# A routed expert block after attention: the last three attention units written out, two banks for turned probabilities, place tables made ahead

## What is computed

```python
z = layernorm(x); z = layernorm(z) * ln_w + ln_b
q, qx, k, v = z @ wq, z @ wqx, z @ wk, z @ wv       # 16 query heads, 8 groups of d = 128
kx, vx = split(ctx @ w_kv_x)                        # q, qx, k and kx are normalised over d
core, xout = gqa(q, k, v), gqa(qx, kx, vx)          # softmax(q @ k.T / sqrt(d)) @ v
x = x + tanh(g_xattn) * (concat(core, xout) @ wproj)
h = layernorm(x)
p = softmax(30 * tanh((h @ w_gate) / 30))           # 8 experts, the top 2 of them for each token
y = sum(p[e] * ((silu(h @ w1[e]) * (h @ w3[e])) @ w2[e]) for e in top2(p))
out = x + tanh(g_ffn) * y
```

## Time and profile before

| | us |
|---|---|
| median of three runs | 717.48 |
| the profiled execution | 719.06 |
| its span, from the first to the last instruction | 717.3 |
| PE busy | 644.7 (90%) |
| DVE busy | 602.9 (84%) |
| ACT busy | 548.0 (76%) |
| POOL busy | 460.1 (64%) |

### The profile page before, as it was taken

How to read it: one execution, slowest core, us unless ns; L and a number is a source line. 1 busy time by engine, 2 the same in 40 slices (tenths; PEclk the granted TensorE clock), 3 DMA queues, 4 the chain that set the end, 5 groups by cost and what they waited for, 6 DMA issues and landing times. The chain is left out here.

```text
span 717.3 us, 14819 instructions
## 1 busy us (share of the span) xinstructions
PE 644.7 (90%) x4548; PEld 589.8 (82%) x4549; DVE 602.9 (84%) x1379; ACT 548.0 (76%) x1923; POOL 460.1 (64%) x636
## 2 busy tenths in 40 slices
PE   1677999999999999999999999999976569999994
PEld 0577889999998999999899999999965448888883
DVE  7579899999999999998999998987876697776771
ACT  4787979998988998998899899888854136656660
POOL 4666677687777778877777787787643124545442
PEclk9989999999999999999999999999999659999998
DMA  6100100010020101002010110100392512232322
GB/s 218 59 1 31 60 1 30 2 59 31 1 61 1 31 2 60 31 1 60 1 32 3 51 42 1 60 1 2 120 397 100 179 64 45 45 58 44 58 31 29
DMA packets 35509, 37.72 MB, mean 53 GB/s; under 512 B 2704, under 2 KB 30352, under 8 KB 35440
## 3 DMA queue, kind: packets, MB, share of 16 engines
q1 hardware_dynamic: 31024, 30.84, 13.0%
q0 software_dynamic: 4416, 6.03, 5.2%
HBM read 31.62 MB, written 5.24 MB: 51 GB/s over the span
## 5 line engine op out<-in xcount | busy, mean ns | idle before, releaser
L1192 POOL TENSOR_SCALAR shared<-shared,rsum 128x256 f32<-128x256 f32 x256 | 143.5, 573 | 67.1 <-DVE rsum L856 61.7
L615 ACT ACTIVATE shared<-s,nmax 128x256 f32<-128x256 f32 x256 | 122.5, 498 | 34.3 <-DVE nmax L851 34.2
L861 DVE TENSOR_TENSOR pt_lo<-t,pt_hi 128x512 fp32r<-128x512 f32 x128 | 86.9, 679 | 9.2 <-ACT pt_hi L621 8.3
L1186 POOL TENSOR_TENSOR rstd<-rstd,half 128x7 f32<-128x7 f32 (+1 forms) x64 | 91.2, 1425 | 5.3
L851 DVE TENSOR_REDUCE nmax<-s 128x2 f32<-128x512 f32 x128 | 86.6, 678 | 5.3 <-PE s L364 4.6
L375 PE MATMUL t<-ident,shared 128*128 128x128 f32 x512 | 78.0, 275 | 8.8 <-DVE pt_lo L861 5.6
L621 ACT CAST pt_hi<-t 128x512 fp32r<-128x512 f32 x128 | 76.4, 597 | 12.3 <-PE t L375 10.0
L629 ACT ACTIVATE shared<-route_bank,head_w 128x512 f32<-128x512 f32 (+1 forms) x124 | 81.6, 690 | 0.3 <-PE route_bank L389 0.3
L846 DVE TENSOR_TENSOR qk_lo<-shared,qk_hi 128x512 fp32r<-128x512 f32 x96 | 78.5, 817 | 3.0 <-POOL qk_hi L1201 1.9
L364 PE MATMUL s<-qk_hi 128*128 128x256 f32 x256 | 78.0, 305 | 0.6 <-ACT shared L615 0.6
L320 PE MATMUL pj_a<-w_ring,xq 128*128 128x256 f32 x488 | 73.8, 295 | 2.2 <-DVE w_ring L927 2.2
(11 more groups left out here) (255 smaller groups left out, 1927.9 us busy)
## 6 DMA issues: line engine op xcount, KB each, us to landing
expert_w<-in_w SPq DMA_DIRECT2D x24, 512.0 KB, 9.3
spare<-in_wT SPq DMA_DIRECT2D x19, 256.0 KB, 3.0
wp_raw<-in_wpT SPq DMA_DIRECT2D x16, 256.0 KB, 2.9
spare<-in_wkvT SPq DMA_DIRECT2D x16, 128.0 KB, 3.1
spare<-in_wT SPq DMA_DIRECT2D x9, 128.0 KB, 3.2
spare<-in_x SPq DMA_DIRECT2D x1, 1024.0 KB, 5.6
x_hat<-acc SPq DMA_DIRECT2D x1, 1024.0 KB, 4.7
out<-spare SPq DMA_DIRECT2D x1, 1024.0 KB, 7.9
```

The costliest lines, as they stand in the source:

```text
L615: e = act.activation(probs[:, st, h * S:(h + 1) * S], s_bank[st][:, h * S:(h + 1) * S], ACT.Exp, bias=nmax[:, st, h:h + 1], accum_out=psum ...
L861: dve.tensor_tensor(pt_lo[:, :, c], pt_bank[:].rearrange("p (n s) -> p n s", n=4), pt_hi[:, :, c].bitcast(F32), ALU.subtract).then_inc(ptl ...
L1186: pool.tensor_tensor(rstd[:, st, c], rstd[:, st, c], half[:, c], ALU.pow).then_inc(rstd_ready, 1)
L1192: m = pool.tensor_scalar(probs[:, st, c], probs[:, st, c], rsum[:, st, h:h + 1], 1.0, ALU.mult, ALU.mult)
```

## The change

1. **Units 29 to 31 are written out** on PE, ACT, DVE and POOL, in another order than `step` gives. In the units 30 and 31 the blocks with st = 1 are turned into `pj_a`, which has no projection left to hold, so `turn_probs` there waits for the block before the last. Some waits are added: `probs_hi` of these units for the values before, `split_heads` and `heads_hi` for the scores before.
2. **The last batch goes by tiles of 128 tokens**: `HATS` has five parts (three batches of two tiles, then one and one). `out_project` of unit 31 writes to the two score banks, `accumulate_last` reads one tile each. `choose` and `rank` go in three parts, `RANKED` (tiles 0 to 3, 4 and 5, 6 and 7).
3. **Place tables of six tiles ahead**: `first_places` (DVE) works out the places of the tiles 0 to 5 within their experts' last 128 before the starts of the experts are known, and POOL makes their twelve 128x128 tables, before the barrier. After it DVE makes those of the last two tiles only, and `id_slot`, which POOL made.
4. **The expert part**: `slot_expert` is worked out ahead of the tokens, `rows_rest(0, 0)` ahead of the scales, `hidden(0, 0, 0)` ahead of `rank_last`. In the loop `turn_hidden(n)` stands between the halves of `hidden(n + 1)` and `down(n)` behind them, where `down(n - 1)` stood between them; ACT and DVE follow.

```diff
+        def turned(u, a, st):
+
+            late = isinstance(u, int) and u >= U - 2 and st == 1
+            return pj_a if late else pt_bank
...
-            for u in range(1, U):
+            for u in range(1, U - 3):
                 step(u // B, u // B % 2, u % B)
...
+                two = isinstance(u, int) and f > 4 * (U - 2)
                 if above(f, 0):
-                    pe.wait_ge(ptlo_done, f)
+                    pe.wait_ge(ptlo_done, f - 1 if two else f)
...
+            turn_probs(31, 1, 0)
+            out_project(G - 1, 1, 2, 30, 0)
+            turn_probs(31, 1, 1)
+            out_project(G - 1, 1, 2, 30, 1)
+            values(31, 3, 1)
             turn_hat(0)
             turn_hat(1)
-            for st in range(ST):
-                out_project(G - 1, 1, B - 1, U - 1, st)
+            logits(0)
+            logits(1)
             turn_hat(2)
...
+            out_project(G - 1, 1, 3, 31, 0, s_bank[0][:, 0:H])
+            out_project(G - 1, 1, 3, 31, 1, s_bank[1][:, 0:H])
...
             def probs_hi(u, a, st):
                 act.wait_ge(pt_done, 4 * u + 2 * a + st + 1)
+                if u > U - 4:
+                    act.wait_ge(pv_done, 2 * u + a)
...
+            hat_copy(0)
+            smooth(G - 1, 31, 1)
+            hat_copy(1)
+            soft_cap(0)
...
+            def accumulate_last(st):
+                dve.wait_ge(tile_out, st + 1)
+                a = acc[:, NT - ST + st, :]
+                dve.tensor_tensor(a, s_bank[st][:, 0:H], a, ALU.add).then_inc(acc_read, 1)
...
+            def first_places():
+
+                dve.wait_ge(counted, 2)
+                n = NT - ST
+                c = slice(0, n)
+                for j in range(TOP):
+                    m = dve.scalar_tensor_tensor(early_pick[:, j, c], route.bank[:, NT * E:(NT + n) * E]
+                                                 .rearrange("p (t e) -> p t e", e=E), -(P - 1) / 2.0, route.pick[:, j, c], ALU.add, ALU.mult)
+                place_link(m)
+                place_link(dve.tensor_reduce(early_row[:, :, c], early_pick[:, :, c], AX, ALU.add))
+                place_link(dve.tensor_scalar(early_slot[:, :, c], early_row[:, :, c], ROWS, ROWS, ALU.add, ALU.subtract))
+                dve.tensor_tensor(early_row[:, :, c], early_row[:, :, c], early_slot[:, :, c], ALU.subtract).then_inc(early_placed, 1)
...
+            pool.wait_ge(early_placed, 1)
+            for t in range(NT - ST):
+                for j in range(TOP):
+                    m = pool.tensor_scalar(early_at[:, j, t, :], route.table[:, T_PLACE:T_PLACE + P], early_row[:, j, t:t + 1], 1.0,
+                                           ALU.is_equal, ALU.mult)
+            m.then_inc(route.places_set, 1)
...
             turn_rows(0, 0)
+            hidden(0, 0, 0)
             rank_last()
-            hidden(0, 0, 0)
             turn_rows(1, 1)
...
                 if more:
                     hidden(n + 1, 1 - par, 0)
-                if least(n, 1):
-                    down(n - 1, 1 - par)
+                turn_hidden(n, par)
                 if more:
                     hidden(n + 1, 1 - par, 1)
-                turn_hidden(n, par)
+                down(n, par)
...
-            for n in range(0, TOP * NT, QUARTER):
-                dve.tensor_tensor(at_place[:, n:n + QUARTER, :],
...
+            for part, v in enumerate((table[:, T_TILE:T_TILE + TOP * NT], off_place[:])):
+                m = dve.tensor_tensor(id_slot[:, part], at_slot[:], over_slots(v), ALU.mult)
+            m.then_inc(identified, 1)
...
+            def step(n, par):
                 more = not isinstance(n, int) or n + 2 < SLOTS
                 if more:
                     rows_rest(n + 2, par)
                     e = expert_of(n + 2)
-                    for i in range(2):
-                        weights_rest(n + 2, par, e, i)
-                if least(n, 1):
-                    take_y(n - 1, 1 - par)
+                    weights_rest(n + 2, par, e, 0)
+                if not isinstance(n, int) or n + 1 < SLOTS:
+                    take_hidden(n + 1, 1 - par)
+                if more:
+                    weights_rest(n + 2, par, e, 1)
+                take_y(n, par)
...
-            pool.wait_ge(sloted, 1)
-            pool.tensor_tensor(id_slot[:, 0], at_slot[:], table[:, T_TILE:T_TILE + TOP * NT].rearrange("p (n o) -> p n o", o=1)
```

More of the change, by code:

```diff
@@ L409, in out_project @@
                         pe.wait_ge(wp_ready, g + 1)
-                    if above(u, 0):
+                    if above(u, 0) and not last:
                         pe.wait_ge(acc_read, u)
@@ L555, in rank @@
                         pe.matmul(to, route.ones[:], route.chosen[:, earlier, :], start=earlier == 0, stop=False)
-                    pe.matmul(to, route.before[:], route.chosen[:, t, :], start=t == 0, stop=True)
+                    m = pe.matmul(to, route.before[:], route.chosen[:, t, :], start=t == 0, stop=True)
+                m.then_inc(counted, 1)
+            steps(step)
+            scores(29, 1, 0, 0)
+            turn_probs(28, 1, 0)
+            out_project(G - 2, 0, 3, 27, 1)
+            scores(29, 1, 0, 1)
@@ new lines, in _ @@
+            turn_heads(30, 2, 0)
+            turn_probs(28, 1, 1)
+            project_q(31, 1, 3, 0)
+            project_kv(31, 1, 3, 0)
+            scores(29, 1, 1, 0)
+            turn_probs(29, 0, 0)
+            values(28, 0, 1)
+            turn_heads(30, 2, 1)
+            scores(29, 1, 1, 1)
+            project_q(31, 1, 3, 1)
+            turn_probs(29, 0, 1)
+            turn_heads(30, 2, 2)
+            project_kv(31, 1, 3, 1)
+            scores(30, 2, 0, 0)
+            values(29, 1, 0)
@@ L1120, in step @@
                 row_sum(u, 1, 1)
-            steps(step)
             chain = [0]
@@ new lines, in _ @@
+            steps(step)
+            quantise(28, 0)
+            normalise_q(30, 2, 1)
+            row_max(29, 0, 0)
+            probs_lo(28, 1, 0)
+            normalise_kv(30, 2, 1)
+            row_max(29, 0, 1)
+            split_heads(29, 1, 2)
+            row_sum(29, 0, 0)
+            probs_lo(28, 1, 1)
+            row_max(29, 1, 0)
+            split_heads(30, 2, 0)
+            row_sum(29, 0, 1)
+            accumulate(27, 3)
+            normalise_q(31, 3, 0)
+            row_sum(29, 1, 0)
@@ L1165, in _ @@
+            probs_lo(31, 1, 1)
+            accumulate(30, 2)
+            x1_tiles(2)
+            quantise(31, 1)
+            x1_normalise(2)
+            choose(0)
+            accumulate_last(0)
+            x1_tiles(3)
+            accumulate_last(1)
+            x1_tiles(4)
+            x1_normalise(3)
+            x1_normalise(4)
+            choose(1)
+            first_places()
+            choose(2)
             dve.tensor_tensor(route.gap[:, :, 0:E], route.cap[:], over_e(route.top[:, :, 0], NT), ALU.subtract)
@@ L1198, in heads_hi @@
                 wait(aff_done, 3 * u + i + 1)
+                if i == 2 and u > U - 4:
+                    wait(scores_done, 4 * u)
                 c = slice(i // 2 * HC, (i // 2 + 1) * HC)
@@ L1806, in _, with early_tiles @@
             scatter(SLOTS - 1, (SLOTS - 1) % 2)
+def early_tiles(early, tiles, experts):
+    n = TOP * tiles
+    at = early[:, 0:n * P // 2].bitcast(BF16).rearrange("p (j t c) -> p j t c", j=TOP, t=tiles)
+    first = n * P // 2
+    pick = early[:, first:first + n * experts].rearrange("p (j t e) -> p j t e", j=TOP, t=tiles)
+    first += n * experts
+    row, slot = (early[:, first + i * n:first + (i + 1) * n].rearrange("p (j t) -> p j t", j=TOP) for i in range(2))
+    return at, pick, row, slot
 def slot_count(tokens, experts):
```

440 lines of the change are left out of this document (302 added, 138 removed).

## The result

| | us | against the kernel before, 95% interval |
|---|---|---|
| kernel before, median of 10 runs | 717.42 (715.47 to 718.95) | |
| changed kernel, median of 10 runs | 715.09 (712.87 to 717.19) | 0.9965 (0.9952 to 0.9978) |
| forecast | 708.3 (704.5 to 712.8) | |

The change gains 2.3 us where 9.2 us were forecast; the time lies above the range. The profiled execution of the changed kernel took 714.06 us with 712.2 us of span, 5.1 us less span than the one before. Part of that is chance: DVE's `accumulate` of unit 26 (I call it the mark) starts at 489.50 us after the change and at 491.71 before it, 2.2 us apart, and up to there the work is the same. In the fourteen traces of this document, with either order of the last units, the mark lies anywhere from 489.50 to 492.53 us. So I count from the mark.

The account below looks back on a forecast made before the run. PE was taken to bound the rounds, DVE the set-up, a chain through all engines the stretch between, one bank's depth the last units. Terms -8.8 + 1.4 + 0.2 - 2.0 = -9.2 us from 717.48 gave 708.3 us, range 704.5 to 712.8.

Parts of the forecast that it names:

- Term 2: From the start of the last values to the barrier's end: 1.4 us lost, with POOL's twelve tables holding the barrier.
- term 1: Last units, up to the start of the last values: -8.8 us, bounds -4.7 to -11.7.
- Term 3: Set-up, from DVE's start after the barrier to the second slot's first `hidden`: +0.2 us, bounds -0.9 to +0.8.
- term 4: Expert rounds and end: rounds stay at 5.19 us, the last scatter starts earlier, -2.0 us, bounds -1.4 to -3.0.
- POOL's tables: Rival at the barrier: a loss from POOL's twelve early place tables; chance 0.12.
- the wait in the rounds: Rival: PE waits at `hidden(n + 1)`'s second half or `down(n)`; 0.5 us a round gives 719.3 us; chance 0.06.

Follow-up runs that it names:

- The probe: Changed kernel plus sets of POOL instructions behind the last scatter, the first ones with nothing else running; 128x128 with bfloat16 output: compare 711 ns, multiply 371 ns.
- e3: Changed kernel with the twelve early tables made by DVE instead of POOL and `rank_last` ahead of `hidden(0, 0, 0)` again; 707.82 us, 0.9862 of the kernel before.
- e6: Changed kernel with `rank_last` ahead of `hidden(0, 0, 0)` again as its only difference, POOL still making the tables; 711.57 us, 0.9922 of the kernel before.

## Why the prediction was wrong

**Term 2 failed, by its price of POOL's tables.** The mechanism was there in the text: POOL, not SP, holds the barrier, 0.45 us (0.35) from its end to DVE's start, `early_placed` at 15.0 us after the last values (14.7), rows ready at 11.7 (11.9), SP's way 18.6 (18.28 + 0.35). Only the 0.33 us per table was wrong: 0.70 us. The upper bound, 0.45 us, lay below it too. I had started from 452 ns for another operation, an add and multiply of 128x128 beside a busy DVE. I scaled it to 0.27 us for POOL alone by the ratio of two times of a wider form, and chose a value between. The probe shows both steps wrong. It has no add and multiply, but its plain multiply of 128x128 with DVE idle takes 0.37 us, not 0.27. And a compare takes 0.71 us: that I took the row of another operation for its price is nearly all of the error. Term 2 was +1.4 us and is +5.5 us. (The lower end of the range was added up wrongly by a little: term 1 at 40.5 us with term 3's lower bound gives 704.7 us, not 704.5.)

The sentence that I drew from the Trainium skill (GPSIMD Engine Reference, Engine selection), elementwise work to VectorE, was right in its advice, and here the trace is far on its side: 1.82 us against 8.38 us for the twelve tables. Its rates were not: about half as fast with two inputs, near line rate with one, where these two forms are 4.6 times apart. The 0.38 us that I worked out from it was too low all the same.

**Term 3 and a part of term 4 failed by the step on `rank_last`.** I wrote that the 2.6 us are "given back" and took the rounds to begin at 20.75 us. They begin at 21.15: `fill_places` started 15.23 us after the restart instead of 14.95, and from there to the second slot's first `hidden` it was 5.92 us, as before (590.36 - 584.44). That is 0.4 us in term 3, within its bounds. What I left out is PE: I followed the lateness to `fill_places` and to DVE's queue, but not to PE, which then stands idle 2.2 us in two places just when its clock has come up, and runs about half of its time from the second slot's first `hidden` to the next turn at half clock. That takes 1.2 us from term 4 (measured from the `hidden` to the last scatter: 121.01 us before, 120.20 after, so -0.8 instead of -2.0). e3 and e6 show it as a whole: 3.3 and 3.5 us for one line's place. So the move of this line cost more than the 1.8 us that terms 3 and 4 together should bring.

**Term 1 was nearly right:** -8.2 us in the pair of profiles, -8.8 forecast, and 2.3 us of waits for `pt_lo` left (4.0 us of waits in all) where the text said near 5. Against the mean of the four executions with the old order (59.0 us) and the nine with the new order (51.4 us) it is -7.7 us: the execution that I took as my base was about 1 us longer than that mean, at a lower clock.

**Term 4's rounds** were right: `down` of two rounds starts 5.16 us apart instead of 5.19, without idle on PE. From the chain that ended last:

```profile
683.97 1.73 PE route_bank L1756 x8
...
689.13 1.73 PE y L1756 x8
```

At the end I had forecast three scatters back to back. Only the last one stands right behind the one before it; those of the slots 20 and 21 wait for their rows.

The sum from the mark: -8.2 + 5.5 + 0.6 - 0.8 = -2.9 us in the profiles, and -2.3 us in the medians. Of what the chances name, *POOL's tables* is what came, beyond every price of term 2; the wait in the rounds did not come. By mechanism the change has three good parts (the last units and the last batch about 7 us, early tables 1.4 to 1.7 us if DVE makes them, rounds 1.4 to 2.0 us) and two bad placements that eat 5.0 and 3.3 us. e3 undoes both and takes 707.82 us: 0.9862 of the kernel before. That this is near the forecast does not bear the forecast out: e3 has no tables on POOL and not the changed place of `rank_last`.

## What to carry to other kernels

Take the price of an instruction from a row with the same operation and the same width, and where there is none, let the range reach to twice the nearest row: a compare on POOL took twice a multiply, and half the width saved only a fifth of a multiply (481 to 375 ns). Ahead of a meeting of all engines, look for an engine that is done early and does the work fast, and give it the work: here DVE, idle for 7.1 us, which makes the twelve tables in 1.82 us. (ACT was idle longer, 8.8 us; no run here made tables on it.) When an instruction moves behind a long one, follow the lateness until it reaches PE, and count there what the clock costs besides the wait.

## What the hardware showed that I had not expected

On POOL a compare of 128x128 takes 711 ns and a multiply 371 ns with bfloat16 output, 722 and 375 with float32, and by an estimate from two widths some 270 ns of a multiply don't depend on its width. POOL's compares all but stood still beside f32 subtractions on DVE: 5.16 us for two. After two waits of PE of 1.22 and 0.99 us the granted clock fell within 0.9 us of the next work and stood at the lower level for some 3 us, at 1.6 us of cost. And the same unchanged stretch of about 59 us took 58.7 to 60.2 us in three executions of one program, and 57.1 us in one of another. Of the busy times only PE's went with it, at granted clocks from 0.94 to 1.00. What a single profile says of such a stretch has an uncertainty of 1.4 us, and perhaps 3, and a part of it is gone again by the next meeting of the engines.
